# Residual additions of three batches moved from VectorE to Pool in a two-block recurrent kernel

## Chip, core and metric

One core of a Trainium2 chip runs the whole kernel in one launch. The metric is the time of one execution on the device in microseconds; three runs of the kernel before gave 431.07, 431.97 and 432.36 us, median 431.97. The core has a matrix engine (TensorE, PE in the profile), VectorE (DVE), ScalarE (ACT), GpSimd (called Pool here and in the code) and SyncE (SP), which issues most DMA transfers. Each engine executes its own instructions in the order in which they are written; they meet at semaphores.

## The reference

The input x is 4 batches of 256 rows (tokens) of 256 numbers. Two blocks of the same form follow each other. With xn the layer-normalised x, s a mixing of tokens and g the SiLU of a sum over four chosen experts per token:

```
xn = layernorm(x)
s = causal_attention_16_heads(xn)      # block 1: rope, softmax, Wo
g = silu(experts(xn))                  # block 1: 16 experts, 4 per token
x = x + s * g                          # the residual of block 1
xn = layernorm(x)
s = linear_attention(xn)               # block 2
g = silu(experts2(xn) + shared(xn))    # block 2: 32 experts, 4 per token, one shared
x = x + s * g
```

The change concerns the `x + s * g` of block 1: it consists of elementwise additions of `s * g` to x, of 128 partitions by 512 numbers for each batch (two tiles of 128 rows).

## The kernel before, in words

A tile is 128 rows; a batch has two, and x lies in `xr` (8 tiles). The experts' weighted rows of block 1 are written to DRAM, sorted by expert. When the last of these tiles are stored, Pool runs `gather_back` (L573 to L584): for each of the four batches b, for r = 0 and 1, for two halves and two tiles it issues an indirect DMA that fetches rows back into token order, 8 for a batch and 32 in all. The first of each goes to a plain copy, the others add to what is there. The rows land in `fsum` and `fsum2`, and four semaphores s_four count them. After that Pool sets `nmr` by a memset (L606) and computes three powers (L610) for the reciprocal deviations of the second normalisation, then starts the gathers of block 2.

At the same time the other engines run the attention of block 1, in a loop over 32 pairs of heads, 8 pairs for a batch. `run_pairs` writes it as a software pipeline: each entry (lag, every, work) runs its work for item v at step u = lag + v * every, and within a step in the order of the list. The numbers of an entry are thus the places of its work in the engine's instruction stream. VectorE's list (L1743) is:

- every step: `smallest` (the row minima of two heads, L1675) and `probs_turned` (a copy of turned probabilities from PSUM, L1684);
- per batch b, at the step given for b = 0 and 8 steps later for each further batch: `row_sums` (12, fsum + fsum2, L1700), `gate0` (13, gate into `fsil`, L1705), `residual` (13, `fsil` times the projected attention, L1711, raises s_s), `add_residual` (15, adds `fsil` to `xr`, L1717, raises s_x1), `row_stats` (17, statistics of the new x by two bn_stats, L1722, waits for s_x1 of at least b + 1);
- towards the end, once each: `row_moments` (steps 30 and 33, the variances for Pool's powers), `rows_ahead` (32 and 34, normalised rows of the next block, L1737), the sums of the last batch (33) and its gate (36).

`fsil` is one buffer for all batches. TensorE's loop has the scores (L1206), the transposes of probabilities (L1231), the attention matmuls (L1249), turning back (L1262, L1268) and the projection (L1276); ScalarE's has the exponentials (L796) and copies. TensorE waits for VectorE's minima (s_mx) and copies (s_pTr). SP issues the weights of block 2 as pairs of heads become attended (s_pv), and some after the last batch's sum of rows (s_sum).

Of the kernel before, what the change touches and what calls it, by code (L numbers as in the profile page):

```python
# [22 lines left out]
BATCH, SEQ = 4, 256  # L23
# [51 lines left out]
def build_program(nc, x, consts, wqkv0, wo0, wr0, rb0, gub0, dnb0, gu0, dn0,  # L75
                  wqvu1, b768, wo1, lnrow, bo1, wr1, gu1, dn1, wsgu, wsdn, out):
    f32, bf16, fp16, i32, u32 = mybir.dt.float32, mybir.dt.bfloat16, mybir.dt.float16, mybir.dt.int32, mybir.dt.uint32
    ALU, ACT, AX = mybir.AluOpType, mybir.ActivationFunctionType, mybir.AxisListType
    ctx = ExitStack()
    with ctx:  # L80
        def sb(name, shape, dt=f32):
            return ctx.enter_context(nc.sbuf_tensor(name, shape, dt))

        def sem(name):
            return ctx.enter_context(nc.semaphore(name))
# [46 lines left out]
        xr = sb("xr", [P, NTT, D])  # L132
# [57 lines left out]
        ftanh, fsil, oTs = (rou[:, at:at + 512].rearrange("p (t n) -> p t n", t=2) for at in (2048, 2560, 3072))  # L190
# [139 lines left out]
        s_x1 = sem("x1_ready")  # L330
# [12 lines left out]
        def ge(eng, s, v):  # L343

            if v > 0:
                eng.wait_ge(s, v)

        def run_steps(total, body, stages):

            for u in range(min(lag for lag, _, _ in stages), total + max(lag for lag, _, _ in stages)):  # L350
                for lag, every, work in stages:
                    v = u - lag
                    if v % every == 0 and 0 <= v < total:
                        work(v // every, v // every % (body // every))
# [158 lines left out]
        @block.gpsimd  # L513
        def _(po):
            chain = [0]

            def link(ins):

                chain[0] += 1
                ins.then_inc(s_pool, 1)  # L520
                po.wait_ge(s_pool, chain[0])

            def gather_tiles(s):

                ge(po, s.xn_stored, 16 * NTT)
                po.wait_ge(s.lists, 1)

                def gather(t):
                    if t >= 4:
                        po.wait_ge(s.xgT_done, t - 3)  # L530
                    po.indirect_dma_start(xg[:, t % 4, :], None, xn_dram[s.n],  # L531
                                          bass.IndirectOffsetOnAxis(ap=gidx[:, t:t + 1], axis=0))\
                      .then_inc(s.xg_full[t % 4], 16)

                for t in range(4):
                    gather(t)
                for t in range(4, s.NT):
                    gather(t)
                    if s.n == 0 and t == 7:
                        po.wait_ge(s.lists, 3)  # L540
                        po.wait_ge(s.wide_read, NTT)
                        po.wait_ge(s_dn0, 80)
                    if s.n == 0 and t >= 7 and (t - 7) % 3 == 0 and (t - 7) // 3 < NTT:
                        rotate((t - 7) // 3)
                    if s.n == 0 and t in (33, 44):
                        a = t // 44
                        po.wait_ge(s_heads[a], 16 * 32)
                        po.memset(vst[:, 4 * a:4 * a + 4, :, DH:DH + 1], 1.0).then_inc(s_vst, 1)
                        po.memset(vst[:, 4 * a:4 * a + 4, :, DH + 1:], 0.0).then_inc(s_vst, 1)

            def rotate(i):

                at = slice(i % 2 * P, (i % 2 + 1) * P)
                ct, st = (rope_cs[:, c, :, at].unsqueeze(1).broadcast_to([P, 2, 2, P]) for c in range(2))
                raw = qkT[:, i // 4, :, :, i % 4 * P:(i % 4 + 1) * P]
                po.tensor_tensor(rtmp, raw, st, ALU.mult).then_inc(s_rst, 1)
                po.wait_ge(s_rst, 2 * i + 1)
                po.tensor_tensor(raw, raw, ct, ALU.mult).then_inc(s_rst, 1)
                po.wait_ge(s_rst, 2 * i + 2)
                po.tensor_tensor(raw[:, 0, :, :], raw[:, 0, :, :], rtmp[:, 1, :, :], ALU.subtract)  # L560
                po.tensor_tensor(raw[:, 1, :, :], raw[:, 1, :, :], rtmp[:, 0, :, :], ALU.add).then_inc(s_rope, 1)
                po.wait_ge(s_rope, i + 1)

            def gather_four(i):

                ge(po, s_f1, i - 3)
                po.wait_ge(s_four[i % 4], 64 * (2 + i // 4))
                for k in range(TOPK):
                    po.indirect_dma_start(fours[i % 4][:, k, :], None, ys_dram[1],
                                          bass.IndirectOffsetOnAxis(ap=slotu[1][:, i * TOPK + k:i * TOPK + k + 1], axis=0))\  # L570
                      .then_inc(s_four[i % 4], 16)

            def gather_back(s):  # L573

                po.wait_ge(s.wexp_out, 2 + BATCH)
                for b in range(BATCH):
                    for r in range(2):
                        for half, rows in ((0, fsum), (1, fsum2)):
                            for i in (2 * b, 2 * b + 1):
                                k = 2 * r + half  # L580
                                ge(po, s_four[i % 2 * 2 + half], 32 * b + 16 * r)
                                po.indirect_dma_start(rows[:, i, :], None, ys_dram[s.n],  # L582
                                                      bass.IndirectOffsetOnAxis(ap=slotu[s.n][:, i * TOPK + k:i * TOPK + k + 1], axis=0),
                                                      compute_op=ALU.add if r or half else ALU.bypass).then_inc(s_four[i % 2 * 2 + half], 16)  # L584

            def tiles_stored(s):
                for j in range(4):
                    po.wait_ge(s.y_stored[j], 16 * ((s.NT - j + 3) // 4))


            link(po.memset(bias_f[:, :], 0.0))
            po.wait_ge(s_cst, 16)
            po.tensor_scalar(iota_m[:, :, :], iota.unsqueeze(2).broadcast_to([P, P, 2]), -63.5, None, ALU.add).then_inc(s_tab, 1)
            po.tensor_scalar(iota_t[:, :, :], iota[:, 0:P // 2].unsqueeze(2).broadcast_to([P, P // 2, 2]), float(P), None, ALU.mult).then_inc(s_tab, 1)

            po.wait_ge(s_wqkv, 16)
            for w in range(2):
                link(po.tensor_copy(wqk_halves[:, :, w, :, :].rearrange("p k f (h d) -> p k f h d", d=HALF),
                                    wqkv_sb[:, :, w * D:(w + 1) * D].rearrange("p k (h f d) -> p k f h d", f=2, d=HALF)))

            gather_tiles(L[0])


            tiles_stored(L[0])
            gather_back(L[0])
            link(po.memset(nmr[:, :], -0.5))  # L606

            for n, (t0, t1) in enumerate(EARLY_ROWS):
                po.wait_ge(L[1].ve_ready, n + 1)
                po.tensor_tensor(rstd[:, t0:t1], sd[:, t0:t1], nmr[:, t0:t1], ALU.pow).then_inc(L[1].sd_ready, 1)  # L610

            gather_tiles(L[1])
            tiles_stored(L[1])
            for i in range(NTT):
                gather_four(i)
# [768 lines left out]
        def _(ve):  # L1384
# [317 lines left out]
            def gate0(b, j):  # L1702

                ve.wait_ge(s_fe, b + 1)
                ve.scalar_tensor_tensor(out=fsil, in0=ftanh, scalar=1.0, in1=fsum[:, 2 * b:2 * b + 2, :], op0=ALU.add, op1=ALU.mult).then_inc(s_sil, 1)  # L1705

            def residual(b, j):
# [4 lines left out]
                                        op0=ALU.mult, op1=ALU.mult).then_inc(s_s, 1)  # L1712

            def add_residual(b, j):
                ve.wait_ge(s_s, b + 1)
                rows = xr[:, bass.ds(b * 2, 2), :]
                ve.tensor_tensor(rows, rows, fsil, ALU.add).then_inc(s_x1, 1)  # L1717

# [21 lines left out]
            def first(work):  # L1740
                return lambda b, j: work(b, j) if b < BATCH - 1 else None

            run_pairs([(0, 1, smallest), (2, 1, probs_turned), (13, 8, first(gate0)), (17, 8, row_stats), (13, 8, residual), (15, 8, add_residual),  # L1743
                       (7, 4, scale_rows), (12, 8, first(row_sums)),
                       (30, ONCE, lambda n, j: row_moments(0)), (32, ONCE, lambda n, j: rows_ahead(0)),
                       (33, ONCE, lambda n, j: row_moments(1)), (33, ONCE, lambda n, j: row_sums(BATCH - 1, j)),
                       (34, ONCE, lambda n, j: rows_ahead(1)),
                       (36, ONCE, lambda n, j: choices(L[1], 0)), (36, ONCE, lambda n, j: gate0(BATCH - 1, j)),
                       (36, ONCE, lambda n, j: picks(L[1], 1))])
            row_moments(2)  # L1750
# [161 lines left out]
```

## Time and profile before

| what | value |
|---|---|
| median of three runs | 431.97 us |
| profiled execution | 431.09 us |
| its span | 429.3 us |
| mean granted clock of TensorE | 0.986 |
| PE busy | 411.7 us, 96% |
| DVE busy | 330.6 us, 77% |
| ACT busy | 236.6 us, 55% |
| POOL busy | 216.7 us, 50% |

The span runs from the first to the last instruction of the profiled execution. Busy shares are over the whole span; the attention of block 1 lies at about 180 to 262 us of it. Times of rows are counted from the start of the span. Where one instruction starts before the recorded end of the one ahead of it on the same engine, the two overlap in the engine's pipeline, so the recorded durations add up to a little more than the time that passes.

### The profile page before, as it was taken

What the parts mean: (1) busy time and instruction counts of PE and PEld (TensorE: products, weight loads), DVE (VectorE), ACT (ScalarE), POOL (GpSimd) and SP (SyncE); (2) the same over time, 40 slices, a digit from 0 to 9 for tenths busy, and PEclk for the clock granted to TensorE, in tenths of its full rate; (3) what the DMA queues carried; (4) which work ended last, traced back from release to release, by engine and by line L of the source; (5) the groups of instructions that cost most, each with busy time, mean ns of one, the idle gap of its engine ahead of it and who ended that gap; (6) DMA issues with size and microseconds to landing.
All of it is one profiled execution on the core that took longest, in us unless ns stands there. A gap on an engine that the chain in (4) does not pass through costs nothing.

```text
span 429.3 us, 10086 instructions
## 1 busy us (share of the span) xinstructions
PE 411.7 (96%) x3213; PEld 319.1 (74%) x3213; DVE 330.6 (77%) x1135; ACT 236.6 (55%) x596; POOL 216.7 (50%) x208
## 2 busy tenths in 40 slices
PE   8999999999999999899999979999999999999995
PEld 4856999889999999766666668547777776566684
DVE  5886889989977766769999998866676766644896
ACT  3283243334533343689999962555676766633731
POOL 2114587777734322077886420067676670477720
PEclk9899999999999999969999999999999999999999
DMA  7947988889999998139877977024555552333312
GB/s 230 395 153 271 329 272 257 269 248 287 290 314 307 291 310 285 64 79 257 179 149 183 232 269 242 1 58 136 165 172 169 166 178 97 97 98 111 99 61 73
DMA packets 42275, 84.17 MB, mean 196 GB/s; under 512 B 7137, under 2 KB 27105, under 8 KB 41585
## 3 DMA queue, kind: packets, MB, share of 16 engines
q1 hardware_dynamic: 30656, 60.99, 43.1%
q0 software_dynamic: 9936, 20.85, 19.0%
q10 hardware_dynamic: 1632, 1.71, 1.2%
q8 instruction: 27, 0.44, 0.4%
q14 instruction: 24, 0.19, 0.1%
HBM read 65.81 MB, written 15.60 MB: 190 GB/s over the span
## 4 chain that ended last, share of the span: by engine, by line
PE 82%; DVE 13%; issue 2%; DMA 1%; ACT 1%; POOL 1%; DVEq 0%
PE ps L1130 16%; PE ps L1081 8%; PE ps L1146 7%; PE ps L1308 6%; PE ps L1231 5%; PE ps L1108 5%; PE ps L1206 3%; PE ps L909 3%; PE ps L1067 3%; PE ps L925 3%; PE ps L1319 3%; PE ps L1119 2%; PE ps L1276 2%; PE ps L898 2%; PE ps L928 1%
## 5 line engine op out<-in xcount | busy, mean ns | idle before, releaser
L531 POOL DMA_INDIRECT til<-xn_rows,gidx x95 | 97.6, 1027 | 102.5 <-PE ps L1119 40.3
L1130 PEld LDWEIGHTS ps<-til,experts 128*128 128x128 f32 x752 | 90.9, 192 | 5.4 <-DVE til L1583 2.2
L1130 PE MATMUL ps<-til,experts 128*128 128x128 f32 x752 | 91.9, 275 | 1.5 <-DVE til L1583 1.5
L695 ACT ACTIVATE til<-ps 128x256 f32<-128x256 f32 x47 | 18.0, 383 | 64.4 <-PE ps L1119 63.6
L743 ACT ACTIVATE til<-ps,wtile 128x256 f32<-128x256 f32 x95 | 42.2, 470 | 13.1 <-PE ps L1110 13.1
L796 ACT ACTIVATE til<-til,mxs 128x128 f32<-128x128 f32 (+1 forms) x128 | 48.9, 451 | 0.0
L1146 PE MATMUL ps<-experts,til 128*128 x188 | 48.4, 381 | 0.0
L1675 DVE CUSTOM_DVE_ANT_0 til<-ps,cst 128x128 f32<-128x128 f32 (+1 forms) x128 | 37.8, 352 | 5.2 <-PE ps L1206 4.5
L1083 PE MATMUL ps<-xn,til 128*64 128x192 f32 x192 | 36.3, 332 | 0.0
L1081 PE MATMUL ps<-experts,til 128*64 x192 | 36.3, 332 | 0.0
L1146 PEld LDWEIGHTS ps<-experts,til 128*128 128x128 f32 x188 | 32.1, 190 | 2.8 <-issue 0.3
L1231 PE MATMUL ps<-cst,til 128*128 128x128 f32 x192 | 29.3, 292 | 4.5 <-DVE til L1684 3.5
L1580 DVE TENSOR_SCALAR til<-ps,bcol 128x128 f32<-128x128 f32 x47 | 16.4, 348 | 20.9 <-PE ps L1130 20.7
L1231 PEld LDWEIGHTS ps<-cst,til 128*128 128x128 f32 x192 | 21.8, 147 | 13.9 <-issue 9.6
L582 POOL DMA_INDIRECT rou<-sorted_rows,slotu x16 | 20.1, 1255 | 22.9 <-DMA sorted_rows<-til 17.5
L1585 DVE SCALAR_TENSOR_TENSOR til<-til 128x256 f32<-128x256 f32 x47 | 28.4, 604 | 1.6
L1081 PEld LDWEIGHTS ps<-experts,til 128*64 128x64 f32 x192 | 24.3, 136 | 7.1 <-issue 4.4
L707 ACT ACTIVATE til<-til 128x256 f32<-128x256 f32 x47 | 19.6, 417 | 17.4 <-DVE til L1581 17.3
L582 POOL DMA_INDIRECT experts<-sorted_rows,slotu x16 | 24.8, 1549 | 8.7 <-DMA experts<-sorted_rows,slotu 4.4
L1591 DVE TENSOR_TENSOR til<-til 128x256 f32<-128x256 f32 x47 | 27.1, 576 | 2.6 <-ACT til L707 0.5
L1308 PE MATMUL ps<-att,experts 128*128 128x512 f32 x64 | 28.6, 594 | 0.0
L1108 PE MATMUL ps<-experts,til 96*64 x96 | 24.7, 379 | 0.7 <-ACT til L743 0.7
(237 smaller groups left out, 913.8 us busy)
## 6 DMA issues: line engine op xcount, KB each, us to landing
experts<-in_gu SPq DMA_DIRECT2D x47, 512.0 KB, 5.7
sorted_rows<-til SPq DMA_DIRECT2D x95, 128.0 KB, 1.9
experts<-in_gu SPq DMA_DIRECT2D x8, 768.0 KB
experts<-in_dn SPq DMA_DIRECT2D x4, 1024.0 KB, 12.6
experts<-in_dn SPq DMA_DIRECT2D x8, 384.0 KB
til<-xn_rows,gidx POOLq DMA_INDIRECT x95
experts<-att SPq DMA_DIRECT2D x44, 32.0 KB
xr<-in_x SPq DMA_DIRECT2D x2, 512.0 KB, 4.1
```

What stands on the lines that cost most here:

```text
L531: po.indirect_dma_start(xg[:, t % 4, :], None, xn_dram[s.n], bass.IndirectOffsetOnAxis(ap=gidx[:, t:t + 1], axis=0))\
L582: po.indirect_dma_start(rows[:, i, :], None, ys_dram[s.n], bass.IndirectOffsetOnAxis(ap=slotu[s.n][:, i * TOPK + k:i * TOPK + k + 1], axis=0),
L743: ac.activation(ybuf[:, j, :], y, ACT.Copy, scale=wtile[:, t:t + 1])\
L796: ins = ac.activation(pr[h % len(pr)][:, cols], pr[h % len(pr)][:, cols], ACT.Exp, bias=mxs[:, h % len(pr), tt:tt + 1], scale=-1.0)
L1081: pe.matmul(ps[0:HALF_ROWS, 2 + p % 2, at], xgT1[:, p % 2, c, k, 0:HALF_ROWS], gu[:, bass.ds(e * (KD * w) + k * w, w)], start=(k == 0), st ...
L1083: mm = pe.matmul(ps[HALF_ROWS:P, 2 + p % 2, at], xgT1[:, p % 2, c, k, HALF_ROWS:P], gu_second[t % 4][:, k * w:(k + 1) * w], start=(k == 0) ...
L1108: pe.matmul(ps[0:HALF_ROWS, 6 + p % 2, at], hT1[:, p % 2, c, 0:HALF_ROWS], dn[0:F1, bass.ds(e * D, D)], start=True, stop=True)
L1130: mm = pe.matmul(ps[:, b0, m * P:(m + 1) * P], gw[:, j, k * w + m * P:k * w + (m + 1) * P], xgT[:, j % 2, k, :], start=(k == 0), stop=(k = ...
L1146: mm = pe.matmul(ps[:, 6 + j % 2, 0:D], hT[0:s.FP, j % 2, k, :], dn[0:s.FP, bass.ds(e * (s.KF * D) + k * D, D)], start=(k == 0), stop=(k = ...
L1231: mm = pe.transpose(ps[:, 4 + h % 2, n * P:(n + 1) * P], pr[h % len(pr)][:, n * P:(n + 1) * P], ident)
L1308: mm = pe.matmul(ps[:, n % 2 + 2 * w, :], wsgu_sb[:, k, w * SH + m * P:w * SH + (m + 1) * P], L[1].xnT[:, k, h * 512:(h + 1) * 512], start ...
L1675: ve.tensor_tensor_reduce(out=pr[h % len(pr)][:, cols], in0=ps[:, h % 4, cols], in1=maskz[:, (1 - tt) * P:2 * P], scale=1.0, scalar=3.0e38 ...
```

## The change

Pool adds `fsil` to `xr` for the batches 0, 1 and 2. The additions for 0 and 1 stand in `gather_back` within the last batch, the first ahead of its four gathers of r = 0, the second ahead of its four of r = 1; that for batch 2 stands behind all gathers, ahead of the memset. Each waits for s_s of at least b + 1 and raises s_x1. VectorE's `add_residual` returns at once for these batches, and for the last it waits for s_x1 of at least 3 too. `gate0`, which overwrites `fsil`, waits for s_x1 of at least b. `row_stats`, the list of VectorE's steps and everything else stay as they are.

```diff
+            def add_residual(b):
+
+                po.wait_ge(s_s, b + 1)
+                rows = xr[:, 2 * b:2 * b + 2, :]
+                po.tensor_tensor(rows, rows, fsil, ALU.add).then_inc(s_x1, 1)
+
             def gather_back(s):
 
                 po.wait_ge(s.wexp_out, 2 + BATCH)
                 for b in range(BATCH):
                     for r in range(2):
+                        if b == BATCH - 1:
+                            add_residual(r)
                         for half, rows in ((0, fsum), (1, fsum2)):
...
             tiles_stored(L[0])
             gather_back(L[0])
+            add_residual(2)
             link(po.memset(nmr[:, :], -0.5))
...
             def gate0(b, j):
 
                 ve.wait_ge(s_fe, b + 1)
+                ge(ve, s_x1, b)
                 ve.scalar_tensor_tensor(out=fsil, ...
...
             def add_residual(b, j):
+                if b < BATCH - 1:
+                    return
                 ve.wait_ge(s_s, b + 1)
+                ve.wait_ge(s_x1, b)
                 rows = xr[:, bass.ds(b * 2, 2), :]
                 ve.tensor_tensor(rows, rows, fsil, ALU.add).then_inc(s_x1, 1)
```

## Rows read from the trace of the kernel before

**Rows 1.** The page: busy us (share of the span) xinstructions, by engine.

```profile
PE 411.7 (96%) x3213; PEld 319.1 (74%) x3213; DVE 330.6 (77%) x1135; ACT 236.6 (55%) x596; POOL 216.7 (50%) x208
```

**Rows 2.** Busy by window: start:end length, engines' us (x instructions), PEclk, DMA share, GB/s.

```profile
218.00:226.00 8.00, 7.72 (x98) 5.62 (x92) 7.85 (x42) 7.84 (x23) 6.48 (x6) 1.00 0.88 180
...
185.38:191.97 6.59, 6.59 (x49) 4.44 (x47) 4.06 (x25) 5.03 (x14) 5.61 (x4) 0.50 0.43 82
...
14.72:18.00 3.28, 3.28 (x9) 2.50 (x9) 2.94 (x22) 0.38 (x1) 0.00 (x0) 0.50 1.02 422
```

**Rows 3.** The chain of waits, 180 to 310 us: start, us, what.

```profile
249.07 0.60 DVE xr L1717
```

**Rows 4.** Pool by time: start, us, instruction, [idle before, what ended it].

```profile
184.09 0.94 POOL L582 DMA_INDIRECT rou<-sorted_rows,slotu  x1 [17.48 <-DMA sorted_rows<-til]
...
224.08 1.54 POOL L582 DMA_INDIRECT experts<-sorted_rows,slotu  x1 [0.30 <-issue]
225.92 0.99 POOL L582 DMA_INDIRECT rou<-sorted_rows,slotu  x1 [0.30 <-issue]
...
232.88 1.54 POOL L582 DMA_INDIRECT experts<-sorted_rows,slotu  x1 [2.83 <-DMA experts<-sorted_rows,slotu]
...
241.53 1.53 POOL L582 DMA_INDIRECT experts<-sorted_rows,slotu  x1 [1.59 <-DMA experts<-sorted_rows,slotu]
242.48 0.70 POOL L606 MEMSET nmr<- 128x8 f32 x1
247.60 1.05 POOL L610 TENSOR_TENSOR rstd<-sd,nmr 128x4 f32<-128x4 f32 x1 [4.42 <-DVE sd L1731]
```

**Rows 5.** VectorE by time, the lines around the residual.

```profile
209.61 0.69 DVE L1711 SCALAR_TENSOR_TENSOR rou<-rou,ps 128x512 f32<-128x512 f32 x1
...
213.52 0.75 DVE L1717 TENSOR_TENSOR xr<-xr,rou 128x512 f32<-128x512 f32 x1
...
217.96 0.74 DVE L1722 BATCH_NORM_STATS2 bnst<-xr 128x6 f32<-128x256 f32 x2
...
227.08 0.69 DVE L1711 SCALAR_TENSOR_TENSOR rou<-rou,ps 128x512 f32<-128x512 f32 x1
...
235.40 0.74 DVE L1722 BATCH_NORM_STATS2 bnst<-xr 128x6 f32<-128x256 f32 x2
...
244.52 0.69 DVE L1711 SCALAR_TENSOR_TENSOR rou<-rou,ps 128x512 f32<-128x512 f32 x1
...
250.68 1.37 DVE L1737 TENSOR_SCALAR xn<-xr,mv,rstd 128x256 f32<-128x256 f32 x4
...
253.81 0.69 DVE L1700 TENSOR_TENSOR rou<-rou,experts 128x512 f32<-128x512 f32 x1
```

**Rows 6.** Pool's groups by line and shape: busy us, mean ns, idle before.

```profile
L556 POOL TENSOR_TENSOR rou<-att,experts 128x512 f32<-128x512 f32 x8 | 10.2, 1278 | 1.7 <-DVE wtile L1561 1.6
...
L561 POOL TENSOR_TENSOR att<-att,rou 128x256 f32<-128x256 f32 x8 | 6.1, 761 | 0.0
```

**Rows 7.** TensorE by time: transposes of probabilities, and one of turned rows.

```profile
185.06 1.35 PE L1231 MATMUL ps<-cst,til 128*128 128x128 f32 x6 [1.00 <-DVE til L1684]
...
187.94 1.54 PE L1231 MATMUL ps<-cst,til 128*128 128x128 f32 x6
...
200.86 0.88 PE L1231 MATMUL ps<-cst,til 128*128 128x128 f32 x6
...
204.99 0.87 PE L1231 MATMUL ps<-cst,til 128*128 128x128 f32 x6
...
220.42 0.85 PE L1231 MATMUL ps<-cst,til 128*128 128x128 f32 x6 [0.26 <-DVE til L1684]
...
234.06 0.85 PE L1231 MATMUL ps<-cst,til 128*128 128x128 f32 x6 [0.42 <-DVE experts L1684]
...
250.36 0.44 PE L1268 MATMUL ps<-cst,stk 128*128 128x128 f32 x2 [0.29 <-DVE stk L1692]
```

## The prediction

> **What bounds the kernel now.** I read the page first: TensorE is busy for 96% of the span, VectorE for 77% [rows 1]. These are averages over stages, and the change touches only the attention of the first block, 180 to 262 us. So I asked for busy times by window. In 218 to 226 us VectorE is busy 7.85 of 8.00 us, TensorE 7.72 [rows 2]: the two hand work to each other in a loop of pairs of heads, and VectorE has 0.15 us in 8 to spare. The chain of waits says the same: in this stretch it goes back and forth between TensorE and VectorE, and the third batch's residual addition stands on it with 0.60 us [rows 3]. Here, then, a microsecond in which VectorE stands still is a microsecond of the kernel, and one that it is spared is worth at most the short gaps that TensorE has behind it. Last I read the two in-order queues that the change ties together, Pool's and VectorE's, by time.
>
> Pool issues gathers without pause: the first at 184.09, the 24th (the last of the third batch) at 224.08 for 1.54 us, the 25th (the first of the fourth batch) at 225.92 [rows 4]. VectorE finishes the first batch's product (L1711) at 209.61 + 0.69 = 210.30, adds it at 213.52 and takes that batch's statistics (L1722) at 217.96; for the second batch these are 227.08 and 235.40 us [rows 5].
>
> **The first batch's addition: a stall.** This is the step that decides. The addition moves behind Pool's 24th gather. But what needs its result stays where it is: `row_stats(0)` is run at step 17 of the loop and waits for the first count of s_x1. Pool cannot give that count before 225.6, and VectorE asks for it at 217.96. VectorE executes in order, so behind this wait stand the next pairs' minima (L1675) and copies (L1684), for which TensorE and ScalarE wait.
> When does Pool give it? The gather ends at 224.08 + 1.54 = 225.62. Pool has not done this addition before. Its nearest operations of the same shape, 128x512 fp32 with two inputs, are the multiplications of L556 with 1278 ns; its additions at half the width take 761 ns (L561) [rows 6]. I take 1.3 us. The bounds: below, 226.3, if the gather frees the engine early, as the memset that is recorded at 242.48 inside a gather of 241.53 to 243.06 suggests [rows 4] (225.04 + 1.28); above, 227.4, if the addition starts only at the cadence of the gathers (225.92) and takes 1.5. Taken: 225.62 + 1.3 = 226.9, and `row_stats(0)` starts at about 227.0 in place of 217.96. That is +9.0 us (8.3 to 9.5). The 0.6 us that VectorE saves at 213.52 only makes it wait 0.6 us longer.
> How much of the 9.0 is hidden? TensorE can finish what it has: the scores and transposes of 218 to 219 and one group of attention matmuls. Its next group, at 220.42, needs a VectorE copy (0.26 us of idle, released by L1684) [rows 7], and this copy is behind the wait. VectorE has no slack to catch up with afterwards (7.85 of 8.00). So all 9.0 reach the end. The gathers need nothing of VectorE at this point, so this is a delay and no deadlock.
>
> **The clock after the stall: +1.4.** TensorE would stand idle from about 220.2 until the statistics (0.7), two minima (1.1) and the copy (0.5) are done, about 229.3. That is 9 us. What does a much shorter pause do here? Up to 185.06 us TensorE waits 1.00 us for a VectorE copy [rows 7], and in 185.38 to 191.97 its granted clock is 0.50, 1.2 GHz in place of 2.4, though it is busy all that time; 14.72 to 18.00 is another such stretch [rows 2]. So after 9 us of idle I expect the half clock when it resumes. The price per microsecond: the transposes of two successive pairs begin at 185.06 and 187.94, 2.88 us apart, at the half clock; at the full clock two pairs take from 200.86 to 204.99, 2.06 us each [rows 7]. Each microsecond at the half clock loses 1 - 2.06/2.88 = 0.28 us. The stretches seen are 3.3 and 6.6 us long; with 5 us, 1.4 us are lost. Bounds: 0, if the clock has not fallen or is back before it matters, and 3.3, if a stretch as long as 6.59 us loses half.
> The Trainium skill ("TensorE: Matmul & The Clock Gate", Terms) prices throttled time at that time by (1 - K/N), which is half of it. The rows show less, 0.28, because at the full clock VectorE, not TensorE, sets the pace. An estimate by the page would be 2.5 us for 5 us, and the forecast 1.1 us later.
>
> **The second and third additions: -0.7.** `add_residual(1)` is queued between the fourth batch's gathers of r = 0 and r = 1. Before, these four end by 232.88 + 1.54 = 234.4. They start 1.3 us late now, but the last of them waited 2.83 us for a transfer to land [rows 4], so they still end by about 234.4. The product of batch 1 then comes at 227.8 + 9.0 + 1.4 = 238.2, so this time it is Pool that waits, and the sum is there at 239.6. `row_stats(1)` asks at 235.40 + 10.4 = 245.8 or 0.5 sooner: no stall. The gathers of r = 1 are queued behind and run from 239.9 to about 247. Before, the last was issued at 241.53 and its rows were summed at 253.81 [rows 4, 5]; now that sum is due at about 263, which leaves 16 us: no wait. `add_residual(2)` waits for the third product, 245.2 + 9.9 = 255.1, and ends at 256.4; `row_stats(2)` comes just ahead of the last sum of rows, so near 262. Behind it stand the memset (0.70) and the first power (L610), which VectorE's variances release at 247.6 + 9.6 = 257.2 [rows 4]: Pool is free at 257.1, just in time. The waits that the change adds to `gate0` and to the last addition find counts long reached.
> What VectorE is spared: L1717 is recorded with 0.75 us [rows 5], of which 0.60 count on the chain [rows 3]. After the second addition TensorE has a gap of 0.42 us that VectorE ends, at 234.06; I count 0.4. After the third it has one of 0.29 at 250.36 [rows 7]; I count 0.3, since beyond that its own transposes are in front. Bounds: 0, if TensorE sets the pace, and 1.2, if both are worth the whole 0.60. SP's queue moves along: its weight loads wait for pairs of heads that are attended (s_pv) and all come later by the same amount.
>
> **The sum.** 9.0 + 1.4 - 0.7 = +9.7 us. The profiled execution took 431.09 us (span 429.3); with this it is 440.8. The median of the three timed runs is 0.9 higher, 431.97, and gives 441.7. I predict 441.4 us, between the two and nearer to the median.
>
> **Rivals.**
> The stall without the clock: TensorE's half-clock stretch falls mostly inside its idle time, or the clock returns at once. For it: the stretch at 185.38 began while TensorE was working again, so the chip doesn't follow at once, and part of this one may pass while nothing runs. Against it: the idle time is nine times as long as the pause before 185.06. Time: 431.97 + 9.0 - 0.7 = 440.3.
> More than one stall: Pool, now waiting for each product in front of its other work, is late with the memset and the first power, and `rows_ahead(0)` and the transposes of the next block wait. For it: the margin worked out above is nil for Pool, and 2 us for VectorE (the power runs from 247.60 for 1.05, its reader starts at 250.68 [rows 4, 5]). Against it: that second margin. With a low clock as long as 6.6 us (1.9 in place of 1.4) and 1 us here: 431.97 + 9.0 + 1.9 + 1.0 - 0.7 = 443.2.
> The other side, faster: the sum for `row_stats(0)` is there in time and the kernel keeps only the saving. Its place is step 17 of the loop; its price would be -0.7, and about -0.3 more for the addition at 213.52, 431.97 - 1.0 = 431.0 us. The point from which it decides: Pool must reach its fourth batch by 216.6, when it is there at 225.6 [rows 4]. Twenty-four gathers would have to be 0.37 us shorter each, or start 9 us earlier, behind tiles that the change doesn't touch. Only if Pool's records, which are rough, run far behind what it does, can this be.
> That the change does less than it says: if VectorE's wait were satisfied by another count. In the code s_x1 is raised by these additions alone, so I give this nothing of its own.
>
> **How the numbers follow.** Forecast 0.62; stall without clock 0.17; more than one stall 0.15; other side 0.04, of which 0.03 faster; 0.02 for anything that hides the stall, as likely within 0.3% as not. A change under 0.3% (1.3 us) cannot be told from none. So faster 0.03, same 0.02, slower 0.95. The range: below, 431.97 + 8.3 - 1.2 = 439.1 with no clock term, less 0.7 for the spread of runs, 438.4; above, 431.97 + 9.5 + 3.3 = 444.8, which I cut to 444.0, since the upper ends do not come together.
>
> **What would show it.** In the changed kernel's profile: one long idle of VectorE, 9 to 10 us, before L1722 at about 217.4, released by Pool's addition at about 227; no idle before the second and third pairs of L1722; TensorE idle about 9 us from 220; a granted clock of 0.5 for 3 to 7 us from about 229 or earlier; Pool's two later additions standing idle before for s_s. The prediction is wrong if VectorE passes L1722 near 218, if TensorE's idle time is well under 8 us, or if the loop after the stall runs at less than 1.9 us a pair and so regains it.

## The result: 3.2% slower, 446.32 us for 431.79 us

The changed kernel takes 446.32 us (median of 4 runs, 445.55 to 446.94), the kernel before 431.79 us beside it (4 runs, 431.07 to 432.36): a ratio of 1.0319, with an interval of 1.0290 to 1.0348. That is +14.5 us where +9.7 were forecast, 4.9 us above the forecast of 441.4 and outside its range (438.4 to 444.0). (In all results the ratio is taken between runs of the same rounds, disturbed ones left out, so it can differ a little from the quotient of the medians.)

The profiled execution of the changed kernel took 446.88 us, span 445.1 us, against 431.09 and 429.3. The page, in the same columns as [rows 1]: TensorE's busy time is the same but for 0.7 us while its share of the span falls from 96% to 92%, so it stood still longer. In the row of clocks, the two slices of 11 us from 222.6 to 244.8 us show 5 and 6 tenths.

```profile
PE 411.0 (92%) x3213; PEld 318.4 (72%) x3213; DVE 329.4 (74%) x1132; ACT 236.2 (53%) x596; POOL 221.3 (50%) x211
...
PEclk9999999999999999999956999999999999999999
```

The waits of 180 to 300 us (engine, line, what released it: us in all, times, longest) have one new long one on each engine. VectorE waits 14.1 us for Pool's addition (L577) ahead of the statistics (L1735, L1722 before). TensorE waits 14.4 us for VectorE's copy, and ScalarE 13.3 us for its minima, both queued behind that wait.

```profile
PE ps L1240 <- DVE til L1693: 18.4, 9, 14.4
POOL xr L577 <- DVE rou L1721: 15.8, 2, 8.7
...
DVE bnst L1735 <- POOL xr L577: 14.1, 1, 14.1
...
ACT til L805 <- DVE mxs L1684: 13.3, 1, 13.3
```

Pool by time, which answers to [rows 4]. The 24th gather is the one at 228.33, the first sum follows it, and the two later sums stand 7.08 and 8.69 us waiting for their products:

```profile
184.93 0.94 POOL L590 DMA_INDIRECT rou<-sorted_rows,slotu  x1 [18.21 <-DMA sorted_rows<-til]
...
199.15 1.54 POOL L590 DMA_INDIRECT experts<-sorted_rows,slotu  x1 [2.70 <-DMA experts<-sorted_rows,slotu]
...
206.54 1.97 POOL L590 DMA_INDIRECT experts<-sorted_rows,slotu  x1 [1.41 <-DMA experts<-sorted_rows,slotu]
...
228.33 1.54 POOL L590 DMA_INDIRECT experts<-sorted_rows,slotu  x1 [0.30 <-issue]
229.32 1.85 POOL L577 TENSOR_TENSOR xr<-xr,rou 128x512 f32<-128x512 f32 x1
231.32 0.99 POOL L590 DMA_INDIRECT rou<-sorted_rows,slotu  x1 [0.16 <-issue]
...
244.39 1.28 POOL L577 TENSOR_TENSOR xr<-xr,rou 128x512 f32<-128x512 f32 x1 [7.08 <-DVE rou L1721]
...
261.56 1.27 POOL L577 TENSOR_TENSOR xr<-xr,rou 128x512 f32<-128x512 f32 x1 [8.69 <-DVE rou L1721]
262.78 0.11 POOL L615 MEMSET nmr<- 128x8 f32 x1
263.88 1.05 POOL L619 TENSOR_TENSOR rstd<-sd,nmr 128x4 f32<-128x4 f32 x1 [0.99 <-DVE sd L1744]
```

VectorE by time, which answers to [rows 5]: the product (L1721, L1711 before) and the statistics.

```profile
209.30 0.69 DVE L1721 SCALAR_TENSOR_TENSOR rou<-rou,ps 128x512 f32<-128x512 f32 x1
...
231.20 0.75 DVE L1735 BATCH_NORM_STATS2 bnst<-xr 128x6 f32<-128x256 f32 x2 [14.07 <-POOL xr L577]
243.62 0.69 DVE L1721 SCALAR_TENSOR_TENSOR rou<-rou,ps 128x512 f32<-128x512 f32 x1 [0.96 <-PE ps L1285]
251.54 0.74 DVE L1735 BATCH_NORM_STATS2 bnst<-xr 128x6 f32<-128x256 f32 x2
...
268.34 0.74 DVE L1735 BATCH_NORM_STATS2 bnst<-xr 128x6 f32<-128x256 f32 x2
```

These rows give a way to cut any of the kernels into three pieces: from the first product to the first statistics, from there to the second product, and from there to the third statistics. The first piece holds the stall, the second its after-effect, the third the savings. Before [rows 5] they are 217.96 - 209.61 = 8.35, 227.08 - 217.96 = 9.12 and, with the third statistics recorded at 252.57, 25.49 us. Changed they are 21.90, 12.42 and 24.72. So the stall costs 13.55 us, what follows it 3.30, and 0.77 come back: +16.1, of the 15.8 us between the spans.

The busy times by window (columns as in [rows 2]) say what the 3.30 are. TensorE does nothing for 4.71 and then 9.72 us; in the second of these rows its granted clock reads 0.50, and it stays 0.50 for another 7.29 us in which TensorE is busy throughout.

```profile
219.24:223.95 4.71, 0.01 (x1) 0.00 (x0) 0.00 (x0) 0.00 (x1) 4.10 (x3) 0.99 0.90 185
223.95:233.67 9.72, 0.00 (x1) 0.03 (x1) 2.47 (x14) 1.14 (x4) 8.26 (x7) 0.50 0.47 72
233.67:240.96 7.29, 7.29 (x51) 5.14 (x52) 5.46 (x29) 3.98 (x11) 3.11 (x2) 0.50 0.33 57
240.96:262.00 21.04, 20.33 (x232) 14.66 (x232) 19.04 (x89) 19.83 (x56) 7.86 (x6) 1.00 0.64 175
```

TensorE by time, the transposes of probabilities as in [rows 7]: at 1.2 GHz two successive pairs are 3.89 and 3.33 us apart.

```profile
217.59 0.87 PE L1240 MATMUL ps<-cst,til 128*128 128x128 f32 x6
233.67 1.51 PE L1240 MATMUL ps<-cst,til 128*128 128x128 f32 x6 [14.42 <-DVE til L1693]
...
237.56 1.54 PE L1240 MATMUL ps<-cst,til 128*128 128x128 f32 x6
...
240.89 0.89 PE L1240 MATMUL ps<-cst,til 128*128 128x128 f32 x6
```

The mechanism is thus the one forecast, with both costs larger. The experiments ask three things: is Pool's place in its queue the cause, or the work that moved; is the slow stretch after the stall really the clock; and which of the sizes belong to the kernel and which to one execution.

### The profile page after: what moved, and what is told of

Its sections match the earlier page's. It is cut to its first block, busy times and chain, and to the rows that moved or that the text cites. A ratio compares the mean times of both kernels' runs of the same rounds, so it can differ in the third digit from the quotient of the medians.

```text
span 445.1 us, 10090 instructions
## 1 busy us (share of the span) xinstructions
PE 411.0 (92%) x3213; PEld 318.4 (72%) x3213; DVE 329.4 (74%) x1132; ACT 236.2 (53%) x596; POOL 221.3 (50%) x211
## 4 chain that ended last, share of the span: by engine, by line
PE 67%; DVE 13%; DMA 7%; POOL 6%; issue 4%; ACT 1%; SPq 1%; DVEq 0%; POOLq 0%; ACTq 0%
PE ps L1139 15%; PE ps L1090 8%; PE ps L1155 6%; PE ps L1317 6%; PE ps L1117 5%; DMA experts<-sorted_rows,slotu 4%; PE ps L934 3%; PE ps L1328 3%; PE ps L1076 3%; POOL experts L590 3%; PE ps L1240 2%; POOL rou L590 2%; PE ps L918 2%; PE ps L1128 2%; DMA experts<-in_gu 2%
## 5 line engine op out<-in xcount | busy, mean ns | idle before, releaser
L805 ACT ACTIVATE til<-til,mxs 128x128 f32<-128x128 f32 (+1 forms) x128 | 49.1, 454 | 13.3 <-DVE mxs L1684 13.3
```

Source lines behind the costliest of these rows:

```text
L805: ins = ac.activation(pr[h % len(pr)][:, cols], pr[h % len(pr)][:, cols], ACT.Exp, bias=mxs[:, h % len(pr), tt:tt + 1], scale=-1.0)
```

## The experiments

Twelve runs were made (some kernels twice, on another chip), in three groups of four, each group on one chip beside the kernel before. On the chip of the first group everything was slower: the kernel before took 466.47 us (median of 19 runs, 461.72 to 474.04). VectorE reached the first product some microseconds later there, while Pool did not, so the stall was shorter. What the first group left open was run again in the others.

### Pool's additions earlier in its queue

In `gather_back`, with the change otherwise as it is:

```
-                        if b == BATCH - 1:
-                            add_residual(r)
                         for half, rows in ((0, fsum), (1, fsum2)):
+                            if (b, r, half) in ((1, 1, 1), (3, 0, 1)):
+                                add_residual(b // 2)
```

> The three additions stay on Pool with all their waits; only the places of the first two change: batch 0's ahead of the last two gathers of batch 1, batch 1's ahead of the second half of batch 3's r = 0. Theory 'the stall at the first statistics is the cause': Pool gives the first count at about 212 to 214 us, VectorE asks for it near 217, so no stall and no half clock after it; the kernel keeps the three savings, about 1 us under the kernel before: 430.5 to 431.5. Rival 'Pool as the place of the additions costs (longer operations, later gathers, shared access to the memory)': the additions are as many and as long as in the changed kernel, so at least a third of its +14.5 us stays: 436 or more.

> The kernel with the first two additions earlier in Pool's queue, once more, on the chip of the other three: theory stall: 0.5 to 1.5 us under the kernel before, and level with the kernel whose statistics are late. Rival: over it by a third of the changed kernel's loss or more.

First chip: 465.32 us for 466.47, ratio 1.0001 (0.9947 to 1.0054). Second chip: 432.79 us (10 runs) for 432.49 (25 runs), ratio 1.0015 (0.9984 to 1.0047). The loss is gone in both; the gain of 0.5 to 1.5 us that was expected on the second chip is too small to show. In the trace from the second chip, first Pool, then VectorE, the sum is there almost six microseconds before the statistics ask for it:

```profile
210.23 1.28 POOL L577 TENSOR_TENSOR xr<-xr,rou 128x512 f32<-128x512 f32 x1 [0.57 <-DVE rou L1721]
```

```profile
217.38 0.74 DVE L1735 BATCH_NORM_STATS2 bnst<-xr 128x6 f32<-128x256 f32 x2
226.64 0.69 DVE L1721 SCALAR_TENSOR_TENSOR rou<-rou,ps 128x512 f32<-128x512 f32 x1
```

From the first statistics to the second product it is 9.26 us, about as before (9.12). Pool's three additions and its waits for the products cost nothing; only their place does.

### The sum late, the statistics later still

The other end of the same wait: Pool's additions stay where the change put them, and VectorE asks later. Three buffers hold the products, so that of VectorE's gates only the last waits for sums. The lines shown are parts of longer ones.

```
+        fsils = [fsil] + [til[:, at:at + 512].rearrange("p (t n) -> p t n", t=2) for at in (4096, 4608)]
...
-                po.tensor_tensor(rows, rows, fsil, ALU.add).then_inc(s_x1, 1)
+                po.tensor_tensor(rows, rows, fsils[b], ALU.add).then_inc(s_x1, 1)
...
-                ge(ve, s_x1, b)
+                if b == BATCH - 1:
+                    ve.wait_ge(s_x1, b)
...
-(17, 8, row_stats),
+(17, 8, lambda b, j: row_stats(b, j) if b >= 2 else None), (29, ONCE, lambda n, j: [row_stats(b, j) for b in (0, 1)]),
```

> The changed kernel with Pool's instructions as they are, but with no early reader on VectorE: the statistics of the batches 0 and 1 are taken at step 29 of the loop in place of 17 and 25, and the product has three buffers, so that the gates of the batches 1 and 2 wait for nothing. Theory stall: nothing waits for Pool, no half clock is added, the savings of 0.6 us three times stay in part: 0.5 to 1.5 us under the kernel before. Rival 'Pool's additions in this place cost by themselves': over the kernel before by at least a third of the loss of the changed kernel beside it.

Measured: 433.32 us (10 runs), ratio 0.9984 (0.9944 to 1.0024): no loss, and no gain that can be measured either. Pool's first sum is as late as in the changed kernel, and the statistics of both batches are taken at 245.63 without waiting. Pool, then VectorE:

```profile
226.33 1.85 POOL L578 TENSOR_TENSOR xr<-xr,rou 128x512 f32<-128x512 f32 x1
```

```profile
245.63 1.40 DVE L1737 BATCH_NORM_STATS2 bnst<-xr 128x6 f32<-128x256 f32 x4
```

So a late sum alone is harmless. With the experiment above, both ways of removing the wait remove the loss.

### The wait alone, without the moved work

The kernel before, with all its additions on VectorE; Pool only raises a count at the place of its first addition, and the first statistics wait for it.

```
+                        if b == BATCH - 1 and r == 0:
+                            po.memset(mark_cell[:, :], 0.0).then_inc(s_mark, 1)
...
                 ve.wait_ge(s_x1, b + 1)
+                if b == 0:
+                    ve.wait_ge(s_mark, 1)
```

> The kernel before with all additions on VectorE. Pool only writes a memset of one column ahead of batch 3's gathers, and VectorE's first statistics wait for it. Theory stall: the whole loss is in this wait; the stall ends about 1.2 us sooner than in the changed kernel (no 1.3 us addition in front), and the three savings of 0.3 to 0.6 are missing: 446.3 - 1.2 + 0.9 = 446 us (444 to 447.5). Rival 'the additions on Pool cost': 432 to 436.

> All additions on VectorE, only the wait of the first statistics for a memset of Pool ahead of batch 3's gathers. Theory: stall (about 1.2 us shorter than in the changed kernel) and clock are the whole loss, and the savings of 0.9 us are missing: level with the changed kernel beside it, 445 to 447. Rival: the additions on Pool are part of the loss: under 442.

First chip: 469.62 us, ratio 1.0114 (1.0073 to 1.0154), with 4.52 us of waiting. Third chip: 445.55 us for 432.92, ratio 1.0303 (1.0240 to 1.0365), beside the changed kernel's 447.1, ratio 1.0345 (1.0278 to 1.0412). VectorE on the third chip:

```profile
228.01 0.75 DVE L1728 BATCH_NORM_STATS2 bnst<-xr 128x6 f32<-128x256 f32 x2 [10.63 <-POOL mark_cell L581]
241.05 0.69 DVE L1715 SCALAR_TENSOR_TENSOR rou<-rou,ps 128x512 f32<-128x512 f32 x1 [1.25 <-PE ps L1280]
```

The wait alone makes the loss of the change: second piece 13.04 us, third 25.49, exactly as before, since here nothing is saved. No addition moved.

### The same kernels again

Both kernels once more, unchanged: the two on the second chip, the changed one on the third as well.

> The changed kernel itself, once more, beside the kernel before on one chip. In the comparisons so far the kernel before took 431.8 us on one chip and 466.5 on another, where the stall at VectorE's first statistics was 4.5 to 5.6 us long in place of 14.1. If the stall is what costs, the loss follows its length: on a chip where the first product comes near 209 us and the 24th gather ends near 229, +14 us; where the product comes at 212 to 216 and the gather ends at 227, +3 to +8 us. If the loss is fixed (additions on Pool), it is +14 on both.

> The kernel before, for a second trace of it. If Pool's 24th gather ends at 225.6 only by the chance of one execution, it ends near 229 here as in the changed kernel's trace (229.9); if it is the change that makes Pool late, it ends near 225.6 again. The time is that of the kernel before.

> The changed kernel as the measure of the other three on their chip: 446 us, 13.5 to 14.5 over the kernel before, with the first statistics at 228 to 231 us.

The changed kernel: 446.24 us, ratio 1.0323 (1.0278 to 1.0367), and 447.1 as above. The kernel before: 433.06 us, ratio 1.0013 (0.9979 to 1.0046). VectorE in the changed kernel on the second chip, and the 24th gather on Pool:

```profile
228.22 0.75 DVE L1735 BATCH_NORM_STATS2 bnst<-xr 128x6 f32<-128x256 f32 x2 [10.21 <-POOL xr L577]
...
241.57 0.69 DVE L1721 SCALAR_TENSOR_TENSOR rou<-rou,ps 128x512 f32<-128x512 f32 x1 [1.56 <-PE ps L1285]
```

```profile
225.35 1.54 POOL L590 DMA_INDIRECT experts<-sorted_rows,slotu  x1 [0.30 <-issue]
```

The three pieces, in microseconds, from the traces; in brackets the difference from the kernel before in its first trace (8.35, 9.12, 25.49):

```
                        first piece      second piece     third piece     span
before, again            8.32 (-0.03)     9.13 (+0.01)    25.49 (0)       432.1
changed                 21.90 (+13.55)   12.42 (+3.30)    24.72 (-0.77)   445.1
changed, again          18.22 (+9.87)    13.35 (+4.23)    24.73 (-0.76)   444.4
changed, third chip     18.40 (+10.05)   13.07 (+3.95)    24.72 (-0.77)   443.7
wait only, third chip   19.03 (+10.68)   13.04 (+3.92)    25.49 (0)       444.2
pool early, second      7.92 (-0.43)     9.26 (+0.14)     24.83 (-0.66)   427.7
```

The stall is 10 us as a rule; the 13.55 of the first trace belong to that execution. There the 24th gather ended at 229.87, against 226.89 and 226.46 in the two repeats and 226.31 in the kernel before again. The rows shown of Pool give most of it: it started 0.84 us later than before, and two of its gathers waited 2.70 and 1.41 us for an earlier transfer to land, where two in the first trace of the kernel before waited 1.10 and 0.35 us.

### The weight loads out of the way

If SP's weight loads of this stretch hold up the landings that Pool waits for, Pool reaches the addition sooner once they are later (parts of one line):

```
-((1, (0,), (0,)), (3, (1,), (1,)), (5, (), (2, 3)), (7, (), (4, 5)), (9,
+((9, (0,), (0,)), (9, (1,), (1,)), (9, (), (2, 3)), (9, (), (4, 5)), (9,
```

> The changed kernel, with the first eight of SP's weight loads (those at s_pv 1, 3, 5 and 7) held until s_pv 9, so that none runs beside the gathers of the batches 0 to 2. In the changed kernel Pool waited 2.7 and 1.4 us for gathers to land and its 24th gather ended at 229.9, where the kernel before had 225.6. Theory 'the weight transfers make the gathers land late, and so the stall is 13 and not 9 us long': no such waits, the 24th gather ends at about 226 (4 us sooner), and the kernel takes 441.5 to 443.5 if the loads are still in time. Rival 'Pool is late for another reason' (its own start, the additions): it still ends near 229, 446 us. If the loads come too late for block 2, a wait for s_w1 shows it.

Measured on the first chip: 469.31 us, ratio 1.0115 (1.0038 to 1.0193), the same as the other stalling kernels there, with 5.30 us of waiting. The 24th gather ended at 226.80:

```profile
225.26 1.54 POOL L590 DMA_INDIRECT experts<-sorted_rows,slotu  x1 [0.30 <-issue]
```

In the two other stalling kernels on that chip it ended at 227.31 and 227.83. But Pool started earlier here: from its first gather to the end of the 24th it took 41.41 us, against 41.46 and 41.53 in those two. This trace has no wait for a landing among these gathers behind the first, but the other two have none as long as 2.70 either (0.72 at most in one, 0.78 in the other), so the lateness that the loads were to explain did not occur on this chip. The run settles nothing. No wait for the held weights shows in block 2.

### TensorE kept busy through the stall

If the slow second piece is the clock, it must vanish when TensorE does not stand still. Extra transposes into a part of a bank that is free at that time and overwritten afterwards, in `turn_probs`, fill the stall; they need nothing that is queued behind VectorE's wait, and nobody reads them.

```
+                if p == 17:
+                    pe.wait_ge(s_oTr, 3)
+                    for _ in range(80):
+                        pe.transpose(ps[:, 7, 0:P], ident, ident)
```

> The changed kernel with 80 transposes of the identity (0.14 us each at the full clock, about 11 us, results unused) on TensorE within its idle time of 14.4 us, ahead of the transposes of pair 17. Theory 'about 3.3 us of the loss are the half clock after the stall' (VectorE's lag grows from 13.2 us at the first statistics to 16.5 at the second product): the granted clock stays at 1.0 behind the stall and the kernel takes 442.5 to 444. Rival 'the lag grows for another reason, such as a refilled loop': 446 us, as in the changed kernel, or above if the 11 us outlast the stall.

> The changed kernel with 80 idle transposes on TensorE inside its waiting time, once more. So far two traces of the changed kernel show that VectorE's lag behind the kernel before grows by 3.3 and 4.2 us between the first statistics and the second product (predicted: 1.4), with the granted clock at 0.50 for some 7 us after TensorE resumes. The first try gave no answer, since on its chip ScalarE and VectorE stood still for 5.1 and 1.7 us for no wait that the profile shows. Theory clock: granted clock 1.0 behind the stall, first statistics to second product 9.2 to 10 us (9.1 in the kernel before, 12.4 and 13.4 in the changed one), and 3 to 4 us less than the changed kernel beside it: 442 to 443.5. Rival 'the loop has to fill again': 12 us or more between the two, no gain. The transposes may outlast the stall by up to 1 us.

On the first chip 470.01 us, ratio 1.0125 (1.0043 to 1.0207). The granted clock stayed at 1.00 behind the stall, but the time gives no answer: the stall was short (5.61 us), and in the second piece ScalarE stood 5.1 us for nothing that the profile shows:

```profile
ACT til L805 <- issue: 5.1, 1, 5.1
```

On the third chip, 442.15 us for 432.92, ratio 1.0243 (1.0184 to 1.0302), 5.0 us under the changed kernel beside it. VectorE, then TensorE:

```profile
229.72 0.75 DVE L1739 BATCH_NORM_STATS2 bnst<-xr 128x6 f32<-128x256 f32 x2 [8.64 <-POOL xr L577]
...
238.85 0.69 DVE L1725 SCALAR_TENSOR_TENSOR rou<-rou,ps 128x512 f32<-128x512 f32 x1
```

```profile
223.12 8.95 PE L1238 MATMUL ps<-cst 128*128 128x128 f32 x80
232.19 0.84 PE L1244 MATMUL ps<-cst,til 128*128 128x128 f32 x6
```

And by window, after VectorE resumes:

```profile
230.00:240.00 10.00, 9.86 (x103) 7.76 (x102) 9.71 (x46) 8.31 (x23) 5.30 (x5) 1.00 0.53 126
```

VectorE still waits 8.64 us, but the granted clock stays 1.00, the transposes of the next pair take 0.84 us in place of 1.51, and the second piece is 238.85 - 229.72 = 9.13 us, as before to 0.01. So the 3.3 to 4.2 us by which the second piece grew are the clock. The filling does not outlast the stall: the transposes of the next pair start 2.47 us after the statistics (232.19 and 229.72), as in the first trace of the changed kernel (233.67 and 231.20). The first piece is 1.75 us shorter than in the changed kernel beside it (16.65 for 18.40), which is not this edit's doing: in this execution VectorE reached its first product 3.7 us later (213.07 for 209.39) and Pool ended its 24th gather 1.9 us later (228.37 for 226.46), so VectorE had less to wait for. Of the 5.0 us between the medians 3.9 are the second piece (13.07 less 9.13); the rest is not accounted for, and the two profiled spans, 440.8 and 443.7, are 2.9 apart.

### A short stall

Pool's first addition four gathers earlier than where the change puts it, to leave a much shorter wait:

```
+                            if (b, r, half) in ((2, 1, 0), (3, 0, 1)):
+                                add_residual(b - 2)
```

> The changed kernel with the first addition ahead of batch 2's r = 1 (four gathers earlier than its fourth batch) and the second within batch 3's r = 0: Pool reaches it near 219.5 and gives the count near 221, VectorE asks at about 217.5. Theory: a stall of 3 to 4 us at the first statistics; TensorE idles for about as long. If the clock falls only after a long idle, it stays up and the loss is 2.5 to 3.5 us less the savings: 434 to 436. If a pause of 3 to 4 us is enough for the half clock, another 2 to 4 us come on top: 437 to 440.

Measured: 438.49 us (435.26 to 439.16) for 432.92, ratio 1.0128 (1.0069 to 1.0188). The profiled execution is the fastest of the four. VectorE in it waited 1.57 us, where 3 to 4 were expected, TensorE 1.92:

```profile
220.44 0.75 DVE L1735 BATCH_NORM_STATS2 bnst<-xr 128x6 f32<-128x256 f32 x2 [1.57 <-POOL xr L577]
...
231.08 0.69 DVE L1721 SCALAR_TENSOR_TENSOR rou<-rou,ps 128x512 f32<-128x512 f32 x1 [0.94 <-PE ps L1285]
```

```profile
222.91 0.85 PE L1240 MATMUL ps<-cst,til 128*128 128x128 f32 x6 [1.92 <-DVE til L1693]
...
225.41 1.54 PE L1240 MATMUL ps<-cst,til 128*128 128x128 f32 x6
```

```profile
224.30:227.70 3.40, 3.40 (x28) 2.23 (x31) 2.84 (x14) 2.07 (x7) 3.04 (x2) 0.53 0.59 83
```

The first piece is 9.57 us (+1.2) and the second 10.64 (+1.5): after a pause of 1.92 us the first transposes still run at the full clock (0.85 us), the next at half (1.54), for some 3.4 us. In this trace the after-effect is as large as the stall ahead of it. The other three runs took 438.28 to 439.16 us, 3 to 4 us longer, and no trace shows why, so that the time falls within the 437 to 440 forecast for a half clock does not prove the size. That a short pause is enough does not hang on this trace alone: in that of the earlier place on the first chip, where nothing waits for Pool, TensorE pauses 1.80 and 1.64 us for VectorE's copies (up to 205.39 and 226.63), and each pause has 3.4 us at 0.50 behind it (206.2 to 209.6 and 226.6 to 230.0). It is not always so: in the run with the later loads a pause of 1.60 us, up to 204.11, has none.

## Why the prediction was wrong in size and right in kind

Two terms of the sum were too small, and both count. In the trace of the result the stall is the larger miss (13.55 us for 9.0, against 3.30 for 1.4 of the clock); in the two repeats, which came to the same loss, it is the clock (4.23 and 3.95 for 1.4, against 9.87 and 10.05 for 9.0).

**The stall at the first statistics, +9.0: right in its mechanism, too small by 1 in the repeats and by 4.6 in the trace of the result.** Place and releaser held. The addition took 231.17 - 229.87 = 1.30 us after the gather's end, 1.3 taken. VectorE passed the wait at 227.8 to 228.2 us in the repeats, with 227.0 forecast. What failed is the distance of the two queues, which was taken from one execution; the bounds (8.3 to 9.5) allowed only for the start and the cost of the addition. The reading "without pause" was wrong too: in that very trace two of the gathers behind the first waited 1.10 and 0.35 us for a transfer to land, and it is such waits that grew to 2.70 and 1.41:

```profile
198.55 0.99 POOL L582 DMA_INDIRECT rou<-sorted_rows,slotu  x1 [1.10 <-DMA rou<-sorted_rows,slotu]
...
213.54 0.97 POOL L582 DMA_INDIRECT rou<-sorted_rows,slotu  x1 [0.35 <-DMA rou<-sorted_rows,slotu]
```

In seven traces (the kernel before twice, the changed one's two repeats, and three of the experiments outside the first group) the 24th gather ended at 225.62 to 228.37, in the first trace of the changed kernel at 229.87; VectorE's first product moved between 208.98 and 213.07. The stall came to 8.3 (16.65 - 8.35, with TensorE kept busy), 9.9, 10.1, 10.7 and 13.6 us.

**TensorE's idle time, 9 us: it follows the stall.** It was 14.42 us in the trace of the result, with a stall of 13.6, and 10.57 and 10.75 us in the repeats.

**The clock, +1.4: the step that failed in every trace.** The clock fell, as forecast, but the term was 3.3, 4.2 and 4.0 us. Both factors were too small. The length: 7.29 us at 0.50 in the trace above and 9.2 and 8.6 in the repeats, where 5 were taken from stretches of 3.3 and 6.6 us [rows 2]. The price: 3.30 / 7.29 = 0.45 us for each, and 0.46 in both repeats, where 0.28 were taken. That price set unlike pairs against each other. The pair of 185.06 to 187.94 us [rows 7] has only transposes of probabilities and scores between its ends, and its first transposes began ahead of the half clock; of the two pairs at the full clock one also has the attention matmuls, the other turning back (L1262):

```profile
190.85 1.45 PE L1231 MATMUL ps<-cst,til 128*128 128x128 f32 x6
...
202.76 0.85 PE L1231 MATMUL ps<-cst,til 128*128 128x128 f32 x6 [0.24 <-DVE til L1684]
203.54 0.66 PE L1262 MATMUL ps<-cst,til 128*128 128x128 f32 x4
```

Pairs with the same work, 187.94 to 190.85 at the half and 200.86 to 202.76 at the full clock, are 2.91 and 1.90 us apart, which is 0.35. After the stall the two pairs are 3.89 and 3.33 apart, while in the repeat of the kernel before the same two take 2.08 and 1.91 (they start at 221.79, 223.87 and 225.78): 0.47 and 0.43. These also carry turning back (L1271, L1277), which is more work for TensorE in a pair that at the full clock VectorE helps to pace. That this is why they lose more is read from the rows and was not tested by itself. The Trainium skill ("TensorE: Matmul & The Clock Gate", Terms) prices throttled time at half of it. That was the better guide here: the runs give 0.45 to 0.46. My upper bound of this term, 3.3, was only just enough for the first trace and too low for the repeats. Why the longest stall has the smallest after-effect, the rows show too: in the three traces of the changed kernel and in that of the wait alone the clock is at 0.50 for the same 17.1 us, idle time included (223.9 to 241.0 in the first, 222.8 to 239.9, 221.8 to 238.9 and 221.9 to 239.1), so a longer idle time uses up more of it.

**The later additions, -0.7: right.** The third piece is shorter by 0.77, 0.76 and 0.77 us in the three traces of the changed kernel, and by nothing where only the wait was added. There was no second stall: the statistics of the second and third batch (251.54, 268.34) show no idle time, Pool stood 7.08 and 8.69 us for its products, and the memset and the first power came in time.

**The sum.** With the sizes of the second chip, 9.9 + 4.2 - 0.8 = +13.3 in the trace, 0.4 us under the 13.75 between the medians there (446.24 against 432.49). Against the forecast of 9.7, the clock carries 2.8 of the difference and the stall 0.9. In the trace of the result it is 13.6 + 3.3 - 0.8 = +16.1, with 4.6 for the stall and 1.9 for the clock; the profiled executions of that pair are 15.8 apart, the medians 14.5. The 14.5 us of the first result are not measurably more (intervals 1.0290 to 1.0348 and 1.0278 to 1.0367).

**The rivals.** The stall without the clock is refuted by the 0.50 in all three traces and by the kernel that kept TensorE busy; its reason was half right, since about half of the stretch at 0.50 (9.72 us of 17.1 in the first trace) passes while nothing runs. More than one stall came nearest with its time (443.2), for a reason that was not so. The other side, a sum in time, is what the earlier place gives: it shows no gain that can be measured (ratio 1.0015, interval 0.9984 to 1.0047), though its trace is 0.95 us shorter over the three pieces, against the 1.0 forecast.

**What stays open.** Why Pool's gathers wait longer for landings in some executions than in others; whether the weight loads have a part in it was not settled. Why one chip ran the kernel before 34 us longer. Why three of the four runs with the short stall took 3 to 4 us more than the one profiled. No kernel tried is measurably faster than the one before.

## What to carry to other kernels

When an operation moves to another engine's in-order queue, compare the time at which that queue reaches it with the time at which its first reader asks, and take both from several executions: one trace carries the cost of an operation, not the distance between two queues. A stall in a loop in which TensorE is nearly always busy brings the half clock after it, to be priced from rows of the same kind of work (here 0.45 us for each of 7 to 9 us), so that even a stall of 1.6 us cost double in the one trace of it. To prove what a wait costs, add the wait alone; to prove the clock, fill the pause.

## What the runs showed of the hardware

- The half clock outlasted the pause by 7.3 to 9.2 us of nearly unbroken work on TensorE after pauses of 10.6 to 14.4 us, and by about 3.4 us after one of 1.92 us, where it fell only when work had begun again.
- The stretch at the half clock near 185 us [rows 2] varies between executions: it is there in 13 of the 14 traces, 3.4 to 10.2 us long (10.2 in the repeat of the kernel before, 6.8 in its first trace), and missing in the first trace of the changed kernel, whose granted clock in the same window is 1.00:

```profile
185.38:191.97 6.59, 5.48 (x70) 3.79 (x71) 5.51 (x31) 6.59 (x21) 5.37 (x5) 1.00 0.43 88
```

- Pool's addition of 128x512 fp32 took 1.27 to 1.30 us where VectorE's takes 0.68 to 0.75 (0.75 in [rows 5]).
- Pool's rows overlap: the addition behind a gather is recorded at 229.32 for 1.85 us while the gather runs to 229.87. The end less the gather's end, 1.30 us, agrees with the additions that stand alone (1.28, 1.27).
